# Expert products of 256 columns, one to a quarter slot, normalisation on ScalarE, and max products ahead of the score product

## The chip, the cores and the metric

The kernel runs on one core of a Trainium2 chip. The metric is the time of one execution in device microseconds, from three runs of the kernel before. A profile is one further execution; its span is measured from the first to the last instruction.

## What is computed

x is 2048 x 256 in float32. Four layers follow each other, each of them on a normalised x and added to x:

```python
x = x + xcond_attention(layernorm(x), ctx, ctx, tau, delta)      # 16 heads of 16, 2048 queries, 1601 keys
x = x + moe_top1(layernorm(x))                                    # 8 experts of 256x256, top one, times its probability
x = x + local_attention(ctx, layernorm(x), lenS2, p_t)            # window of 256 keys, tanh([context, x] @ W_c.T)
x = x + slot_layer(layernorm(x))                                  # router to 64 slots (top 8), GRU, slot attention
def moe_top1(x):
    probs = softmax(x @ router_w.T + router_b)
    top1, weights = argmax(probs), max(probs)
    y_all = einsum('bsd,eod->bseo', x, expert_w) + expert_b
    return y_all[top1] * weights
def layernorm(x): return (x - mean(x)) / sqrt(var(x) + 1e-5)
```

## The kernel before

The 2048 tokens are worked on in four chunks of 512 (four tiles of 128). For each chunk the attention of the first layer runs through 52 **slots**: four groups of four heads, and in each group 13 blocks of up to 128 keys. A slot has four **quarters**, one for each head, so a chunk has 208 quarters. In each quarter TensorE computes a score product into one of two PSUM banks (L977, bf16, 512 columns), ScalarE takes its exponential (L616), and one or two **max products** (L735, bf16, 401 columns) of the next group are computed, whose row maxima VectorE takes (L1125) from a ring of three PSUM banks. The max of a row of scores is subtracted later through two extra rows of the score product. Five max products fall on most slots. At the end of a slot TensorE computes the products of the probabilities of the slot before with the values (`pv`, L814, float32, four at a time on 32 columns each). A score product waits until the exponential two quarters before has left its bank; a max product waits until the reduction three before is done.

The rest of the layers (attention output, router, experts, local attention, slot router) is the **work behind**: the generator `behind(c - 1)` of each engine, which is woven between the quarters of chunk c. So chunk 0 carries none, chunks 1 to 3 carry that of chunks 0 to 2, and that of chunk 3 runs alone after the loop, which is called the tail here. `JOBS` is a table of numbers that sets where each product of it stands: name, the job it follows, the lag in quarters, and how many quarters its PSUM bank is held. `places()` turns it into a quarter for each job (`AT`), since all these jobs share two PSUM banks in turn. A step `yield AT[...] + n` on an engine means: go on when the loop has come to that quarter. On TensorE the work behind stands after the score product and the max products of its quarter, on VectorE after the reductions of the quarter, on ScalarE after the exponential. Each engine runs its own instructions strictly in the order written.

Jobs by name: `ota`, `otb` turn the attention output, `y0`, `y1` are its output products; `t1a`, `t1b` turn the normalised x (tile `xn`) for the router and the experts, `t2a`, `t2b` for the local attention, `t3a`, `t3b` for the slot router; `e0` to `e15` are the expert products, two experts for one tile of tokens each (L880), which VectorE adds with the gate as a factor (L1254), at four and five quarters after the job's place; `gateT` and `gb0`, `gb1` add the experts' biases; `score0`, `score1`, `z0`, `z1` belong to the local attention; `h` has a Gelu on ScalarE, `logits`, `slots` and `alphaT` belong to the slot router. Two more jobs are fixed: `o` (turning the head outputs, at quarters 6, 58, 110, 162) and `m` (turning the maxima, at 45, 97, 149, 201).

A normalisation takes statistics on VectorE (L1199, L1203), the factor 1/sqrt(var + eps) on GpSimd (`rsqrt`, L524 and L526), and then four VectorE instructions that write `xn` (L1117, `normal`), all four in one quarter.

## Time and profile before

| | us |
|---|---|
| median of three runs | 1205.0 |
| lowest, highest | 1202.1, 1208.08 |
| the profiled execution | 1201.54 |
| its span | 1199.9 |
| TensorE, VectorE, ScalarE, GpSimd busy | 1021.9, 809.4, 562.3, 44.1 |

The profiled execution took 1201.54 us, of which 1.6 us lie outside its span, and is 3.5 us under the median. The start (loading, projections, the first maxima) takes 146 us, chunk 0 takes 167 us, chunks 1 to 3 take 239 to 241 us each, and 165 us come after them. A matmul of 512 columns in float32 shows as two records of TensorE. Busy times of overlapping records are counted once.

### The profile page before, as it was taken

The numbers are of one execution on the slowest core, as the hardware profiler recorded it, in microseconds if no ns is written. First come the engines' busy times: TensorE is split into PE (matmuls) and PEld (weight loads), VectorE is DVE, ScalarE is ACT, GpSimd is POOL, SyncE is SP. The second block draws the span as 40 slices with busy tenths as digits, with TensorE's granted clock in tenths as the row PEclk, the third lists the DMA queues.
The fourth block names the chain that finished last, engine by engine and source line by source line (L and its number), as shares of the span: only waits on it lengthen the run. The fifth ranks groups of instructions, "written<-read, shape, count | busy, mean of one in ns | idle before, by whom it ended". The sixth has DMA issues, their size and how long they took to land.

```text
span 1199.9 us, 13638 instructions
## 1 busy us (share of the span) xinstructions
PE 1021.9 (85%) x4812; PEld 411.0 (34%) x4812; DVE 809.4 (67%) x1820; ACT 562.3 (47%) x1019; POOL 44.1 (4%) x54
## 2 busy tenths in 40 slices
PE   6446999999988998988899989888999898696656
PEld 3322233232333333433433334333333343243424
DVE  4446978787767777777677777776777677644232
ACT  4121066667644545666445556664455466301210
POOL 3110000000000000000000000000000000100000
PEclk9876599999989999999899999998999899978665
DMA  8996000000100000001000000010000000100512
GB/s 248 146 112 220 1 1 14 15 1 14 33 1 14 1 14 1 14 1 49 1 14 1 14 1 14 1 49 1 14 1 14 1 15 1 49 0 1 146 49 70
DMA packets 44238, 40.65 MB, mean 34 GB/s; under 512 B 10109, under 2 KB 42334, under 8 KB 43914
## 3 DMA queue, kind: packets, MB, share of 16 engines
q1 hardware_dynamic: 41594, 38.17, 13.6%
q10 hardware_dynamic: 2496, 1.35, 0.8%
q8 instruction: 38, 0.62, 0.2%
q0 software_dynamic: 80, 0.26, 0.2%
q14 instruction: 30, 0.25, 0.1%
HBM read 29.52 MB, written 10.59 MB: 33 GB/s over the span
## 4 chain that ended last, share of the span: by engine, by line
issue 46%; PE 26%; DVE 11%; DMA 6%; SPq 5%; ACT 2%; DVEq 2%; POOL 2%; POOLq 0%; ACTq 0%
DVE mx L1125 8%; PE ps_o L814 7%; PE ps_e L977 7%; PE ps_m L735 6%; DMA k_parts<-alphaT 2%; SPq L395 2%; DMA k_stack<-q_stack 2%; DMA xres<-in_x 1%; SPq L443 1%; PE ps_m L1040 1%; ACT probs L616 1%; PE ps_m L926 1%; SPq L419 1%; PE ps_m L929 1%; DMA x<-xres 1%
## 5 line engine op out<-in xcount | busy, mean ns | idle before, releaser
L1125 DVE TENSOR_REDUCE mx<-ps_m 128x1 f32<-128x401 f32 x1102 | 578.0, 568 | 203.7 <-PE ps_m L735 196.2
L616 ACT ACTIVATE probs<-ps_e 128x512 f32<-128x512 f32 (+1 forms) x832 | 472.6, 597 | 405.6 <-PE ps_e L977 404.8
L735 PE MATMUL ps_m<-k_stack,q_stack 99*128 99x401 bf16 x1102 | 356.7, 353 | 40.8 <-DVE mx L1125 40.0
L977 PE MATMUL ps_e<-q_stack,k_stack 101*128 101x512 bf16 (+1 forms) x832 | 326.2, 392 | 8.3 <-ACT probs L616 6.2
L814 PE MATMUL ps_o<-probs,v_heads 128*32 128x512 f32 (+1 forms) x1664 | 226.9, 618 | 0.0
L977 PEld LDWEIGHTS ps_e<-q_stack,k_stack 101*128 101x128 bf16 (+1 forms) x832 | 82.6, 99 | 302.1 <-ACT probs L616 207.5
L735 PEld LDWEIGHTS ps_m<-k_stack,q_stack 99*128 99x128 bf16 x1102 | 109.9, 100 | 175.9 <-DVE mx L1125 124.8
L880 PE MATMUL ps_m<-expert_w,xnT 128*128 128x512 f32 x256 | 130.8, 612 | 16.2 <-DVE xb L1254 16.2
L1254 DVE SCALAR_TENSOR_TENSOR xb<-ps_m,hot,xb 128x256 f32<-128x256 f32 x112 | 54.1, 483 | 18.3 <-PE ps_m L880 9.2
L880 PEld LDWEIGHTS ps_m<-expert_w,xnT 128*128 128x128 f32 x256 | 47.7, 196 | 48.3 <-DVE xb L1254 24.7
L814 PEld LDWEIGHTS ps_o<-probs,v_heads 128*32 128x32 f32 (+1 forms) x1664 | 33.0, 108 | 64.7 <-issue 56.1
L626 ACT COPY xnT<-ps_m 128x512 f32<-128x512 f32 x24 | 14.1, 586 | 48.7 <-PE ps_m L832 48.7
L832 PE MATMUL ps_m<-ident,xn 128*128 128x128 f32 x96 | 20.5, 321 | 17.4 <-DVE xn L1117 17.4
L524 POOL TENSOR_TENSOR var_e<-mv,eps 128x4 f32<-128x4 f32 x16 | 3.2, 199 | 698.3 <-DVE mv L1203 651.8
L763 PE MATMUL ps_m<-expert_w,probs 128*128 128x256 f32 (+1 forms) x52 | 13.8, 419 | 14.6 <-DVE v_heads L1087 14.6
L832 PEld LDWEIGHTS ps_m<-ident,xn 128*128 128x128 f32 x96 | 15.5, 170 | 23.4 <-DVE xn L1117 18.6
L723 PE MATMUL ps_e<-probs,expert_w 128*128 128x512 f32 (+1 forms) x32 | 14.5, 601 | 9.8 <-DMA probs<-in_ctxT 9.6
L552 POOL TENSOR_TENSOR xres<-xres,bo 128x1024 f32<-128x1024 f32 x4 | 9.4, 2355 | 357.6 <-DMA xres<-in_x 357.6
L926 PE MATMUL ps_m<-win_v,work 128*128 128x256 f32 x64 | 19.6, 400 | 1.9 <-ACT work L626 1.9
L842 PE MATMUL ps_m<-win_k,xnT 128*128 128x256 f32 x64 | 18.3, 422 | 2.1 <-issue 1.4
L929 PE MATMUL ps_m<-wc,xnT 128*128 128x256 f32 x64 | 19.1, 392 | 0.0
L723 PE MATMUL ps_e<-xnT,expert_w 128*128 128x512 f32 x32 | 16.3, 657 | 3.1 <-ACT xnT L597 3.1
(215 smaller groups left out, 617.3 us busy)
## 6 DMA issues: line engine op xcount, KB each, us to landing
q_stack<-q_parts SPq DMA_DIRECT2D x114, 64.0 KB, 2.2
k_stack<-k_parts SPq DMA_DIRECT2D x18, 256.0 KB, 14.0
q_parts<-attn_chunk SPq DMA_DIRECT2D x6, 384.0 KB, 5.8
...
```

The costliest lines, as they stand in the source:

```text
L395: eng.dma_start(qst[16 * (j + i):16 * (j + i) + 16, g, :, :], src.rearrange("(h e) t -> e h t", h=HG))\
L616: act.activation(probs[0:n, k % 2, h, :], ps_e[h % 2][0:n, :], ACT.Exp).then_inc(s["exp_done"], 1)
L723: mm = pe.matmul(ps_e[m][:, 0:n], wqkv[:, w, k, P * m:P * m + P], src[:, k, at_col:at_col + n], start=(k == 0), stop=(k == KT - 1))
L735: pe.matmul(ps_m[:, (UNITS * n1 + u) % RING, 0:SPLIT], qst[0:MAX_ROW, g, h, P * t:P * t + P], kst[0:MAX_ROW, HG * g + h, QUARTER_START[q]: ...
L814: mm = pe.matmul(ps_o[32 * h:32 * h + 32, :], v_sb[0:n, st, HG * g + h, :], probs[0:n, k % 2, h, :], start=(st == 0), stop=(st == ST - 1))
L832: mm = pe.transpose(bank(name, c)[:, P * t:P * t + P], src[:, t, P * k:P * k + P], ident[:])
L880: mm = pe.matmul(bank(name, c), xnT[:, k, P * t:P * t + P], expert_w[:, k, CT * j:CT * j + CT], start=(k == 0), stop=(k == KT - 1))
L926: pe.matmul(o, aT[:, k, tok:tok + P], win_v[:, k, :], start=(k == 0), stop=False)
L929: mm = pe.matmul(o, xnT[:, k, tok:tok + P], wc[:, KT + k, :], start=False, stop=(k == KT - 1))
L977: pe.matmul(ps_e[h % 2][0:n, :], kst[0:ROWS, HG * g + h, P * st:P * st + n], qst[0:ROWS, g, h, :], start=True, stop=True).then_inc(s["qk_r ...
L1125: dve.tensor_reduce(mx[:, q, col:col + 1], ps_m[:, (UNITS * n1 + u) % RING, 0:SPLIT], AX.X, ALU.max)\
L1254: last = dve.scalar_tensor_tensor(out=xb[:, t, :], in0=bank(f"e{i}", c)[:, D * (e % 2):D * (e % 2) + D], scalar=hot8[:, t, e:e + 1], in1=( ...
```

## The change

The numbers of `JOBS` are new, and so are these parts:

- On TensorE the max products of a quarter stand ahead of its score product, not behind it, and the work behind comes after the score product.
- An expert job was two float32 products of 512 columns, at its quarter and two quarters later. It is now four of 256 columns, in four quarters in a row. `y0`, `y1`, `score0`, `score1` were two products in each of two quarters, and are now one in each of four.
- `gb0` and `gb1` stand after `e2` (before: after `e15`), and VectorE adds their result there, to `xa` for the tiles whose experts have not begun. The statistics for the second normalisation of a tile are taken as soon as its four expert jobs are added.
- The three normalisations of the work behind write `xn` on ScalarE: out = Identity(rstd * x + off), two instructions in each of two quarters, the first pair three quarters ahead of `t1a`, `t2a` and `t3a`. The offset -mean * rstd is computed by GpSimd in three more instructions after the factor. The statistics of the first and third stand one in each quarter rather than two.
- The work behind of a chunk may reach into the next one: `AT` goes up to 216, and quarters from 208 on are carried out in the next chunk's first quarters.

```diff
-JOBS = [("ota", None, 10, 3), ("otb", "ota", 2, 3), ("y0", "otb", 3, 3), ("y1", "y0", 2, 3), ("t1a", "y1", 11, 3),
-        ("t1b", "t1a", 2, 3), ("router", "t1b", 3, 2), ("e0", "router", 5, 6)]
-JOBS += [(f"e{i}", f"e{i - 1}", 4, 6) for i in range(1, 4)] + [("gateT", "e3", 3, 3), ("e4", "gateT", 1, 6)]
-JOBS += [(f"e{i}", f"e{i - 1}", 4, 6) for i in range(5, NE)]
-JOBS += [("gb0", f"e{NE - 1}", 4, 4), ("gb1", "gb0", 2, 4), ("t2a", "gb1", 11, 3), ("t2b", "t2a", 2, 3),
-         ("score0", "t2b", 3, 3), ("score1", "score0", 2, 3), ("aTa", "score1", 13, 3), ("aTb", "aTa", 2, 3),
-         ("z0", "aTb", 3, 9), ("z1", "z0", 8, 9), ("t3a", "z1", 20, 3), ("t3b", "t3a", 2, 3), ("h", "t3b", 3, 5),
-         ("logits", "h", 6, 2), ("slots", "logits", 14, 6), ("alphaT", "slots", 4, 3)]
+JOBS = [("ota", None, 9, 3), ("otb", "ota", 2, 3), ("y0", "otb", 3, 6), ("y1", "y0", 4, 6), ("t1a", "y1", 16, 3),
+        ("t1b", "t1a", 2, 3), ("router", "t1b", 3, 2), ("e0", "router", 4, 6), ("e1", "e0", 4, 6), ("gateT", "e1", 4, 3),
+        ("e2", "gateT", 1, 6), ("gb0", "e2", 4, 4), ("gb1", "gb0", 2, 4), ("e3", "gb1", 2, 6)]
+JOBS += [(f"e{i}", f"e{i - 1}", 4, 6) for i in range(4, NE)]
+JOBS += [("t2a", f"e{NE - 1}", 13, 3), ("t2b", "t2a", 2, 3),
+         ("score0", "t2b", 3, 6), ("score1", "score0", 4, 6), ("aTa", "score1", 13, 3), ("aTb", "aTa", 2, 3),
+         ("z0", "aTb", 3, 9), ("z1", "z0", 8, 9), ("t3a", "z1", 21, 3), ("t3b", "t3a", 2, 3), ("h", "t3b", 3, 5),
+         ("logits", "h", 6, 2), ("slots", "logits", 12, 6), ("alphaT", "slots", 4, 3)]
 
...
     fixed = sorted([(q, q + 3) for q in O_AT] + [(q, q + 2) for q in M_AT])
+    fixed += [(HG * SLOTS + q, HG * SLOTS + end) for q, end in fixed]
...
         for q in range(HG * SLOTS):
+            if c >= 2:
+                order += [(name, c - 2) for name in AT if AT[name] == HG * SLOTS + q]
             if c:
...
-        if c:
-            order += [(name, c - 1) for name in AT if AT[name] >= HG * SLOTS]
+    order += [(name, NC - 2) for name in AT if AT[name] >= HG * SLOTS]
...
+            def shift():
+
+                pool.tensor_tensor(mean_2[:], mv[:, :, 0], neg_half[:], ALU.mult)
+                pool.drain()
+                pool.tensor_tensor(mean_2[:], mean_2[:], rstd[:], ALU.mult)
+                pool.drain()
+                pool.tensor_tensor(off[:], mean_2[:], mean_2[:], ALU.add).then_inc(s["off_ready"], 1)
+
...
+                    shift()
...
+            def normal(src, at, n):
+
+                for t in range(TT):
+                    yield at + t // 2
+                    if t == 0:
+                        act.wait_ge(s["off_ready"], n)
+                    last = act.activation(xn[:, t, 0:D], src[:, t, :], ACT.Identity, bias=off[:, t:t + 1],
+                                          scale=rstd[:, t:t + 1])
+                last.then_inc(s["xn_ready"], 1)
+
...
+                yield from normal(xa, AT["t1a"] - 3, 3 * c + 1)
...
+                yield from normal(xb, AT["t2a"] - 3, 3 * c + 2)
...
+                yield from normal(xres, AT["t3a"] - 3, 3 * c + 3)
...
-                work = begin(behind(c - 1)) if c else None
+            def chunk(c, work):
+                old, work = work, begin(behind(c - 1)) if c else None
...
                         exp(c, k, h)
+                        go_on(old, HG * (SLOTS + k) + h)
                         go_on(work, HG * k + h)
-                go_on(work, NEVER - 1)
-
+                return work
...
                 for i, t in enumerate(tiles):
-                    if i:
-                        yield AT[name] + i
                     for k in range(KT):
+                        yield AT[name] + KT * i + k
                         mm = pe.matmul(bank(name, c)[:, D * i:D * i + D], rows[:, k, P * t:P * t + P], weights[:, k, :],
                                        start=(k == 0), stop=(k == KT - 1))
                 filled(mm, name, c)
...
                     bank_free(pe, name, c)
-                    for k in range(KT):
-                        yield AT[name] + 2 * k
-                        mm = pe.matmul(bank(name, c), xnT[:, k, P * t:P * t + P], expert_w[:, k, CT * j:CT * j + CT],
-                                       start=(k == 0), stop=(k == KT - 1))
+                    for n in range(2):
+                        for k in range(KT):
+                            yield AT[name] + KT * n + k
+                            mm = pe.matmul(bank(name, c)[:, D * n:D * n + D], xnT[:, k, P * t:P * t + P],
+                                           expert_w[:, k, CT * j + D * n:CT * j + D * n + D],
+                                           start=(k == 0), stop=(k == KT - 1))
                     filled(mm, name, c)
...
-                for i in range(2):
-                    name = f"gb{i}"
-                    yield AT[name]
-                    wait_taken(pe, "gateT", c)
-                    bank_free(pe, name, c)
...
+                    for m in range(2 if i == 2 else 0):
+                        name = f"gb{m}"
+                        yield AT[name]
+                        wait_taken(pe, "gateT", c)
+                        bank_free(pe, name, c)
+                        for t in range(2):
+                            yield AT[name] + t
+                            mm = pe.matmul(bank(name, c)[:, D * t:D * t + D], gateT[:], eb[:, 2 * m + t, :],
+                                           start=True, stop=True)
+                        filled(mm, name, c)
...
                         pe.wait_ge(m_loaded[g], 32 * (c + 1))
                     for h in range(HG):
+                        for j, u in units_at(k, h):
+                            max_unit(u, c, j)
                         need(pe, s["exp_done"], HG * SLOTS * c + HG * k + h - 1)
                         pe.matmul(ps_e[h % 2][0:n, :], kst[0:ROWS, HG * g + h, P * st:P * st + n],
                                   qst[0:ROWS, g, h, :], start=True, stop=True).then_inc(s["qk_ready"], 1)
-                        for j, u in units_at(k, h):
-                            max_unit(u, c, j)
+                        go_on(old, HG * (SLOTS + k) + h)
                         go_on(work, HG * k + h)
...
-                    if t % 2 == 0:
-                        yield at + t // 2
+                    yield at + t
                     dve.bn_stats(bst[:, t, :], src[:, t, :])
-                yield at + 2
+                yield at + TT
...
-                yield AT["y0"] + 2
+                yield AT["y0"] + 4
                 dve.wait_ge(s["xres_ready"], c + 1)
                 take_sum(xa[:, 0:2, :], xres[:, 0:2, :], "y0", c)
-                yield AT["y1"] + 2
+                yield AT["y1"] + 4
                 take_sum(xa[:, 2:4, :], xres[:, 2:4, :], "y1", c)
-                yield AT["y1"] + 3
-                yield from spread_stats(xa, AT["y1"] + 3)
-                yield AT["t1a"] - 4
-                normal(xa, NC + 3 * c + 1)
+                yield from spread_stats(xa, AT["y1"] + 5)
...
-                dve.drain()
+                    if i == 2:
+                        yield AT["gb0"] + 3
+                        dve.drain()
+                        wait_filled(dve, "gb0", c)
+                        dve.tensor_tensor(xb[:, 0, :], xb[:, 0, :], bank("gb0", c)[:, 0:D], ALU.add)
+                        taken(dve.tensor_tensor(xa[:, 1, :], xa[:, 1, :], bank("gb0", c)[:, D:2 * D], ALU.add), "gb0", c)
+                        yield AT["gb1"] + 3
+                        take_sum(xa[:, 2:4, :], xa[:, 2:4, :], "gb1", c)
+                    if j == 3:
+                        yield AT[f"e{i}"] + 6
+                        dve.drain()
+                        dve.bn_stats(bst[:, t, :], xb[:, t, :])
+                dve.drain()
+                for t in range(TT):
+                    last = dve.bn_aggr(mv[:, t, :], bst[:, t, :])
+                last.then_inc(s["var_ready"], 1)
...
-                yield AT["t3a"] - 3
-                normal(xres, NC + 3 * c + 3)
```

The positions (`AT`) that come out of the table, in quarters of a chunk:

```
before: ota 10 otb 12 y0 15 y1 17 t1a 28 t1b 30 router 33 e0 38 e1 42 e2 48 e3 52 gateT 55 e4 58 e5 64 e6 68 ... e12 92
        e13 98 e14 102 e15 106 gb0 112 gb1 114 t2a 125 t2b 127 score0 130 score1 132 aTa 145 aTb 147 z0 150 z1 158
        t3a 178 t3b 180 h 183 logits 189 slots 203 alphaT 207
after:  ota 9 otb 11 y0 14 y1 18 t1a 34 t1b 36 router 39 e0 43 e1 49 gateT 53 e2 55 gb0 61 gb1 63 e3 65 e4 69 ... e10 93
        e11 99 e12 103 e13 107 e14 113 e15 117 t2a 130 t2b 132 score0 135 score1 139 aTa 152 aTb 154 z0 157 z1 166
        t3a 187 t3b 189 h 192 logits 198 slots 210 alphaT 216
```

How this stands in the engines' own order is shown at three places. The first is TensorE in a chunk with work behind, at an expert job, before: L977 is the score product, L735 the max product, L880 half of an expert job.

```order
L814 MATMUL ps_o<-probs,v_heads 32x512 x4
L977 MATMUL ps_e<-q_stack,k_stack 128x512
L735 MATMUL ps_m<-k_stack,q_stack 128x401
L880 MATMUL ps_m<-expert_w,xnT 128x512
L977 MATMUL ps_e<-q_stack,k_stack 128x512
L735 MATMUL ps_m<-k_stack,q_stack 128x401 x2
L977 MATMUL ps_e<-q_stack,k_stack 128x512
L735 MATMUL ps_m<-k_stack,q_stack 128x401
L880 MATMUL ps_m<-expert_w,xnT 128x512
L977 MATMUL ps_e<-q_stack,k_stack 128x512
L735 MATMUL ps_m<-k_stack,q_stack 128x401
L814 MATMUL ps_o<-probs,v_heads 32x512 x4
```

And the same engine after the change, where L764 is the max product, L1010 the score product, L909 a quarter of an expert job and L843 the product with the values.

```order
L843 MATMUL ps_o<-probs,v_heads 32x512 x4
L764 MATMUL ps_m<-k_stack,q_stack 128x401
L1010 MATMUL ps_e<-q_stack,k_stack 128x512
L909 MATMUL ps_m<-expert_w,xnT 128x256
L764 MATMUL ps_m<-k_stack,q_stack 128x401 x2
L1010 MATMUL ps_e<-q_stack,k_stack 128x512
L909 MATMUL ps_m<-expert_w,xnT 128x256
L764 MATMUL ps_m<-k_stack,q_stack 128x401
L1010 MATMUL ps_e<-q_stack,k_stack 128x512
L909 MATMUL ps_m<-expert_w,xnT 128x256
```

The last max product of a slot no longer stands between its last score product and `pv`, and the first one stands between `pv` and the first score product.

The second place is VectorE at the first normalisation of the work behind, before (L1125 is the reduction of a max product):

```order
L1125 TENSOR_REDUCE mx<-ps_m 128x1
L1203 BN_AGGR mv<-bst 128x2 x4
L1125 TENSOR_REDUCE mx<-ps_m 128x1 x2
L1117 TENSOR_SCALAR xn<-xa,mv,rstd 128x256 x4
L1125 TENSOR_REDUCE mx<-ps_m 128x1 x13
```

After, the four instructions are on ScalarE, among the exponentials (L629); `pv_done` among the waits marks the first exponential of a slot:

```order
L629 ACTIVATE probs<-ps_e 128x512 [waits qk_ready] x3
L647 ACTIVATE xn<-xa,off,rstd 128x256 [waits off_ready]
L647 ACTIVATE xn<-xa,off,rstd 128x256
L629 ACTIVATE probs<-ps_e 128x512 [waits qk_ready,pv_done]
L647 ACTIVATE xn<-xa,off,rstd 128x256 x2
L629 ACTIVATE probs<-ps_e 128x512 [waits qk_ready] x3
```

One pair stands between two slots, the other after the first exponential of a slot.

The third place is ScalarE at the Gelu of job `h`, before, with L616 as the exponential:

```order
L616 ACTIVATE probs<-ps_e 128x512 [waits qk_ready,pv_done]
L616 ACTIVATE probs<-ps_e 128x512 [waits qk_ready] x3
L672 ACT_TABLE_LOAD
L672 ACTIVATE hT<-ps_m,hbias 128x512 [waits bank_filled1]
L616 ACT_TABLE_LOAD [waits qk_ready]
L616 ACTIVATE probs<-ps_e 128x512 [waits pv_done]
```

After, with L698 as the Gelu:

```order
L629 ACTIVATE probs<-ps_e 128x512 [waits qk_ready,pv_done]
L698 ACT_TABLE_LOAD
L698 ACTIVATE hT<-ps_m,hbias 128x512 [waits bank_filled1]
L629 ACT_TABLE_LOAD
L629 ACTIVATE probs<-ps_e 128x512 [waits qk_ready] x3
```

The Gelu with its two table loads stood between two slots, and stands now after the first exponential of one. The number of table loads is unchanged.

## Rows read from the trace of the kernel before

**Rows 1.** The page, first part: busy time, share, instructions of each engine.

```profile
PE 1021.9 (85%) x4812; PEld 411.0 (34%) x4812; DVE 809.4 (67%) x1820; ACT 562.3 (47%) x1019; POOL 44.1 (4%) x54
```

**Rows 2.** Timeline, ScalarE: first exponential of chunk 2, and the loop's end.

```profile
554.80 0.60 ACT L616 ACTIVATE probs<-ps_e 128x512 f32<-128x512 f32 x1 [0.80 <-PE ps_e L977]
...
1035.43 0.58 ACT L680 COPY alphaT<-ps_m 64x512 f32<-64x512 f32 x1
```

**Rows 3.** Timeline of a light slot (chunk 0): start, duration, engine, line, idle before.

```profile
213.93 2.17 ACT L616 ACTIVATE probs<-ps_e 128x512 f32<-128x512 f32 x4 [0.95 <-PE ps_e L977]
...
215.07 0.39 PE L977 MATMUL ps_e<-q_stack,k_stack 101*128 101x512 bf16 x1
...
215.56 1.06 PE L814 MATMUL ps_o<-probs,v_heads 128*32 128x512 f32 x8
...
216.56 0.39 PE L977 MATMUL ps_e<-q_stack,k_stack 101*128 101x512 bf16 x1
...
217.05 2.17 ACT L616 ACTIVATE probs<-ps_e 128x512 f32<-128x512 f32 x4 [0.95 <-PE ps_e L977]
```

**Rows 4.** Timeline, ScalarE: first exponentials of slots full of expert, then of z products.

```profile
640.23 0.60 ACT L616 ACTIVATE probs<-ps_e 128x512 f32<-128x512 f32 x1 [0.95 <-PE ps_e L977]
...
644.79 0.60 ACT L616 ACTIVATE probs<-ps_e 128x512 f32<-128x512 f32 x1 [0.95 <-PE ps_e L977]
...
731.81 0.59 ACT L616 ACTIVATE probs<-ps_e 65x512 f32<-65x512 f32 x1 [1.40 <-PE ps_e L977]
...
736.38 0.60 ACT L616 ACTIVATE probs<-ps_e 128x512 f32<-128x512 f32 x1 [1.39 <-PE ps_e L977]
```

**Rows 5.** Windows of chunk 2: length, busy PE, PEld, DVE, ACT, POOL, granted clock.

```profile
576.00:601.20 25.20, 21.96 (x113) 8.97 (x111) 17.45 (x46) 12.27 (x24) 1.22 (x2) 0.86 0.00 0
692.60:710.80 18.20, 15.30 (x86) 6.10 (x85) 13.74 (x33) 9.93 (x18) 1.21 (x2) 1.00 0.00 0
```

**Rows 6.** Timeline at the first normalisation of the work behind, VectorE and TensorE.

```profile
581.55 1.38 DVE L1117 TENSOR_SCALAR xn<-xa,mv,rstd 128x256 f32<-128x256 f32 x4 [0.53 <-POOL rstd L526]
...
583.47 0.34 PE L735 MATMUL ps_m<-k_stack,q_stack 99*128 99x401 bf16 x1 [1.84 <-DVE mx L1125]
```

**Rows 7.** Timeline at expert job e4, which waits for its bank.

```profile
622.44 0.48 DVE L1254 SCALAR_TENSOR_TENSOR xb<-ps_m,hot,xb 128x256 f32<-128x256 f32 x1
...
622.98 1.13 PE L880 MATMUL ps_m<-expert_w,xnT 128*128 128x512 f32 x2 [1.50 <-DVE xb L1254]
```

**Rows 8.** Timeline, ScalarE, around the Gelu: last exponential before, first ones after.

```profile
768.78 0.60 ACT L616 ACTIVATE probs<-ps_e 128x512 f32<-128x512 f32 x1 [0.23 <-PE ps_e L977]
...
772.69 1.09 ACT L616 ACTIVATE probs<-ps_e 128x512 f32<-128x512 f32 x2
```

**Rows 9.** Groups of instructions by form, ScalarE: shapes, count, busy us, mean ns.

```profile
L654 ACT ACTIVATE work<-work,st 128x256 f32<-128x256 f32 x16 | 7.9, 494 | 0.0
...
L585 ACT ACTIVATE work<-ps_e,qk_bias,tau 128x512 f32<-128x512 f32 x8 | 6.2, 777 | 9.9 <-PE ps_e L723 9.9
...
L585 ACT ACTIVATE work<-ps_e,qk_bias 128x512 f32<-128x512 f32 x6 | 4.1, 682 | 3.0 <-DVE alphaT L1056 2.5 <-DVE win_i L1075 0.5
```

**Rows 10.** Timeline of the tail: a normalisation, then the second one's statistics.

```profile
1047.78 0.20 POOL L524 TENSOR_TENSOR var_e<-mv,eps 128x4 f32<-128x4 f32 x1 [3.74 <-DVE mv L1203]
1048.12 1.02 POOL L526 TENSOR_TENSOR rstd<-var_e,neg_half 128x4 f32<-128x4 f32 x1
1049.17 1.38 DVE L1117 TENSOR_SCALAR xn<-xa,mv,rstd 128x256 f32<-128x256 f32 x4 [1.47 <-POOL rstd L526]
...
1091.85 1.40 DVE L1199 BATCH_NORM_STATS2 bst<-xb 128x6 f32<-128x256 f32 x4
```

**Rows 11.** Timeline of the tail: float32 products of 256 columns back to back.

```profile
1117.94 0.84 PEld L929 LDWEIGHTS ps_m<-wc,xnT 128*128 128x128 f32 x4
1118.15 1.03 PE L929 MATMUL ps_m<-wc,xnT 128*128 128x256 f32 x4
...
1119.02 1.03 PE L926 MATMUL ps_m<-win_v,work 128*128 128x256 f32 x4
```

54 lines of the change are left out of this document (26 added, 28 removed).

## The prediction

> **What bounds the kernel now.** I read the page's first part, then the starts of ScalarE's exponentials (one for each quarter, so they give every slot's length), then the timeline of single slots. TensorE is the busiest engine, at 85% of the span, with VectorE at 67% and ScalarE at 47% [rows 1]. No share tells what an edit is worth, since three kinds of slot lie behind it.
>
> A **light slot** (chunk 0, and those of later chunks that carry nothing) takes 3.12 us, from one first exponential to the next [rows 3]. It is a chain: the last score product waits for the exponential two quarters back, 0.49 us later `pv` starts, 1.00 us after that comes the first score product, 0.49 us later its exponential, and two exponentials later the chain closes. ScalarE idles 0.95 us in each, so none of the engines is full.
>
> A **full slot** takes 4.56 us with two expert products of 512 columns and 4.57 us with four z products of 256 columns [rows 4]. Here TensorE never waits. The float32 passes do 0.87 us for four records of 256 columns at full clock [rows 11], so 0.43 us a product and 1.72 us a slot, whether it is two long products or four short ones.
>
> A **stalled slot** is one in which an engine does a burst. Chunks 2 and 3 together take 480.6 us, 240.3 each [rows 2]. I summed the two kinds of slot over a chunk by what each quarter carries and got 207 us, so about 33 us of a chunk are stalls: TensorE waiting for VectorE or ScalarE, and half clock after such waits. These 33 us, three times, are what the change can move. What lies before the loop stays.
>
> **Expert products in quarters: nothing.** A full slot is 4.56 us with either form [rows 4]. The stalls of this part come from elsewhere: where `o` or `m` breaks the row of jobs, the next expert job uses the bank that VectorE empties one quarter before. e4 waits so for 1.50 us [rows 7], its idle time is paid in full, and five such places (e2, e4, e5, e13, gb0) cost about 8.5 us a chunk by the slots' lengths. The new table has six (e1, e2, gb0, e3, e11, e14). I price each by the VectorE work between the slot's first max product and the emptying (0.5 us for a reduction or an addition, 0.8 for the division of the attention output): 0.6, 1.65, 1.4, 0.9, 1.9 and 1.4 us, with bias sums and clock 8.9 in all. So -0.35 us, a loss, between 3 better and 3 worse.
>
> A rule speaks against this part. Before it, the row: four z products' weight loads of 0.21 us lie inside the running passes, which follow each other at 0.22 us [rows 11]. The Trainium skill, page "TensorE: Matmul & The Clock Gate", section "The mechanism" under packing, says that a weight load overlaps a running matmul only if it goes to other rows of the array. By that, 256 more loads of 0.21 us would stand open, 54 us. The row contradicts it for this very shape, and the sum goes by the row.
>
> **Normalisation: the gain.** The four VectorE instructions stand in one quarter, 1.38 us, and TensorE waits 1.84 us for the ring behind them [rows 6]. The five slots from 576.0 take 25.2 us at a granted clock of 0.86 [rows 5]; by their content (two light, the four turns, the router, half an expert job) they would take 18.4. Of the 6.8 us, statistics and copies keep about 3.2 in the new order. On ScalarE an instruction on 256 columns with one operand per row takes 494 ns, and a second such operand adds 95 ns (777 against 682) [rows 9]; consecutive ones overlap by about 0.09, so 0.50 us each and 1.0 a pair. The pair between two slots lies in the 0.95 us that ScalarE idles [rows 3]; the pair after the first exponential pushes the chain by 1.0. Gain 3.8 us a chunk (2 to 6). At the second one the four slots from 692.6 take 18.2 us [rows 5] against 14.6 by content; its statistics go into full slots, where VectorE has room. One pair's 1.0 and the copies remain: gain 1.2 (0 to 2.5). At the third the pairs stand in quarters 0 and 1, neither between slots, and GpSimd's factor and three more instructions (2.7 us from statistics to offset, by 0.34 for each start [rows 10]) leave three quarters just enough: a loss of 0.6 (-1.5 to +0.5).
>
> **The Gelu.** From the last exponential before it to the next one pass 3.9 us [rows 8], 3.3 of them two table loads and the Gelu. Between slots 0.95 is hidden. After the first exponential of a slot nothing is: a loss of 0.8 us a chunk (0.5 to 2, if the longer wait lowers the clock).
>
> **Order and places.** With the max product ahead, the first one (0.18 us) lies between `pv` and the score product, and the last one (0.17 of the 0.49) leaves the other end; with the two of quarter 1 ahead of its score product the second exponential is 0.04 later. Sum +0.02 us a light slot (-0.05 to +0.06): +1.3 us for chunk 0. In chunks 1 to 3 a product in quarter 0 now pushes the second exponential by its whole 0.43 us and not by 0.29. With that, the contents of a chunk sum to 208.2 us against 207: -1.2 a chunk. The output products, one a quarter, gain 0.4 of the DVE's lag, but `ota` a quarter earlier waits for the division of the same slot, 0.9: -0.5.
>
> **The ledger of a wrapped chunk**: +3.8 + 1.2 - 0.6 - 0.8 - 0.35 - 1.2 - 0.5 = +1.55, and +0.45 for the half clock in 0.86's neighbours, since chunks 1 and 3 have slots there up to 1 us longer: +2.0 us, three times **-6.0 us**.
>
> **Behind the loop.** In the tail everything is open. The offset adds 0.95 us (three starts of 0.34 less overlap) and the four ScalarE instructions take 2.07 against 1.38 [rows 9, 10]: +1.65 us each time. At the second, the 1.40 us of statistics shrink to one of four [rows 10] and the bias sums leave the end, against two products and their sums among the expert jobs: +1.0. Sum **+4.3 us** (3 to 6). The slot products of chunk 2's work now run after the last quarter: **+0.5**.
>
> **Sum**: -6.0 + 1.3 + 4.3 + 0.5 = +0.1 us on the profiled 1201.5, so no change. The profiled execution is 3.5 us under the median of 1205.0, and the same ratio on the median gives **1205 us**, with 1199 to 1211 as this case's own range. About 0.5% (6 us) is what a measurement can tell from no change.
>
> **Rivals.** (1) *Faster*: the bursts were the root of more than their own slots, and ScalarE hides both pairs. Then the first two stretches fall to 0.8 us above content (6.0 and 2.8 gained), the third loses nothing, and the bank waits gain 1. Per chunk 6.0 + 2.8 - 0.8 + 1.0 - 1.7 = 7.3, three times -22, plus 6.1: -16 us, 1189; half way, 1193. For it: a wait of 1.84 us of TensorE [rows 6] in a stretch whose clock is 0.86 [rows 5], so one burst costs twice. Against it: VectorE keeps its statistics and additions. Chance 0.33 for anything under 1199, with 1193 its middle.
> (2) *Slower*: ScalarE runs its instructions in order, and the wait for the offset stands among the exponentials. It decides as soon as the statistics end less than 2.7 us before ScalarE gets there. VectorE is late by an addition or a normalisation of the heads, ScalarE then stops, score products stop, and max products behind them. At 1 us of wait and both pairs open, 1.9 us more at nine places, +17 us: 1218 on the profiled execution, 1222 on the median, and 1214 with half of the places. For it: only three or four quarters lie between. Against it: when VectorE is late, the ring of three holds TensorE and so ScalarE back too. Chance 0.22.
> (3) *Half clock after the Gelu*: TensorE idles some 2.7 us there; if the clock halves as after the wait of rows 6, 3.4 to 6.8 us at half speed, 1.5 to 3 us, three times, 1209 to 1214. Chance 0.08, half of it beyond 1211.
> (4) The edits do nothing: the order of the instructions shows them moved, so this is only the case that stalls wander whole, which my forecast holds. Open weight loads, by the rule above, 1255: 0.02.
>
> My own sum has 0.35. So faster 0.33, same 0.39 (0.35 and half of (3)), slower 0.28. The range of eight in ten takes in most of (1) and part of (2): 1189 to 1219.
>
> **What would show it.** Chunk 0 at 168 to 169 us, light slots of 3.14; full slots of 4.57 with records of 256 columns; the stretch of the first normalisation at about 21 us with clock near 1; ScalarE instructions for `xn` of 0.59 us; a Gelu slot near 8 us; waits for L1254's bank at six places; the tail 4 us longer. A light slot over 3.2 or under 3.0 us would move chunk 0 by more than 3 us and break the sum; so would waits on the offset over 0.5 us, or the loss of the bank waits.

## The result and the profile after

The changed kernel takes **1240.2 us** (median of four runs, 1235.6 to 1241.93), beside it the kernel before 1206.54 us (1202.1 to 1208.21): 1.0281 times as long, 95% interval 1.0249 to 1.0314. Forecast were 1205 us and a range of 1189 to 1219. The loss is outside both.

I read the profile of after in the order of the prediction. First the starts of ScalarE's exponentials (start, duration, engine, line, operation, what it waited for), to hold against [rows 2] and [rows 4]: chunk 0 starts at 144.60, chunk 1 at 312.10, chunk 2 at 555.08, chunk 3 at 808.02, and two neighbouring full slots with four expert products at 650.01 and 654.58.

```profile
144.60 0.60 ACT L629 ACTIVATE probs<-ps_e 128x512 f32<-128x512 f32 x1 [41.35 <-PE ps_e L1010]
312.10 1.08 ACT L629 ACTIVATE probs<-ps_e 128x512 f32<-128x512 f32 x2 [0.96 <-PE ps_e L1010]
555.08 1.08 ACT L629 ACTIVATE probs<-ps_e 128x512 f32<-128x512 f32 x2 [0.40 <-PE ps_e L1010]
650.01 0.60 ACT L629 ACTIVATE probs<-ps_e 128x512 f32<-128x512 f32 x1 [1.39 <-PE ps_e L1010]
654.58 0.60 ACT L629 ACTIVATE probs<-ps_e 128x512 f32<-128x512 f32 x1 [1.39 <-PE ps_e L1010]
808.02 1.08 ACT L629 ACTIVATE probs<-ps_e 128x512 f32<-128x512 f32 x2 [0.40 <-PE ps_e L1010]
```

So chunk 0 takes 167.5 us (before 167.4), chunk 1 243.0 (241.0), chunk 2 252.9 (239.5), chunk 3 254.1 (241.1), and what follows the last exponential 175.2 (164.4). The start is 1.8 us shorter; over the kernels of this case it ends between 144.6 and 149.9 us, so this says nothing about the change. Light and full slots are as before. Of the 37.4 us between the two spans (1237.3 and 1199.9), 26 lie in chunks 2 and 3 and 10.8 in the tail.

Next the same stretches of chunk 2, cut at slots 0, 6, 12 and 17, then slots 36, 44, 48 and the end, first before and then after. Columns: stretch and its length, busy time of TensorE, its weight loads, VectorE, ScalarE and GpSimd, each with its instructions, then the granted clock of TensorE (1.00 is 2.4 GHz, 0.50 is 1.2 GHz), the busy share of the DMA and its GB/s.

```profile
554.80:579.80 25.00, 23.30 (x131) 9.56 (x130) 17.87 (x38) 14.81 (x27) 2.36 (x1) 1.00 0.09 31
579.80:609.60 29.80, 27.11 (x136) 10.86 (x134) 20.83 (x54) 14.78 (x28) 1.22 (x2) 0.89 0.00 1
609.60:635.70 26.10, 22.52 (x107) 8.19 (x107) 17.21 (x35) 12.03 (x23) 0.00 (x0) 1.00 0.06 16
...
723.40:757.40 34.00, 32.14 (x182) 14.67 (x180) 25.04 (x57) 20.70 (x37) 1.21 (x2) 1.00 0.05 12
757.40:775.80 18.40, 16.09 (x94) 6.92 (x93) 12.01 (x25) 13.13 (x21) 0.00 (x0) 1.00 0.00 1
775.80:794.30 18.50, 15.94 (x83) 4.75 (x82) 14.76 (x42) 10.39 (x21) 0.00 (x0) 1.00 0.09 22
```

```profile
555.10:588.60 33.50, 30.18 (x143) 11.86 (x141) 19.04 (x40) 15.88 (x28) 2.34 (x1) 0.85 0.10 34
588.60:614.80 26.20, 23.32 (x137) 9.69 (x136) 19.18 (x52) 16.46 (x31) 1.79 (x5) 1.00 0.01 1
614.80:645.40 30.60, 27.64 (x120) 11.90 (x119) 17.59 (x36) 12.29 (x22) 0.00 (x0) 0.83 0.05 14
...
732.50:768.50 36.00, 32.31 (x182) 14.89 (x181) 24.47 (x54) 22.86 (x46) 0.00 (x0) 1.00 0.04 12
768.50:786.80 18.30, 15.16 (x77) 4.79 (x76) 12.56 (x30) 11.87 (x22) 1.77 (x5) 0.91 0.00 1
786.80:808.00 21.20, 18.39 (x87) 7.37 (x88) 13.76 (x40) 13.41 (x23) 0.00 (x0) 0.84 0.06 17
```

The first normalisation (second row) gained 3.6 us. Slots 0 to 5 lost 8.5, slots 12 to 16 lost 4.5, slots 36 to 43 lost 2.0, slots 48 to 51 lost 2.7. Where it lost most, the clock column fell. Summed over chunks 1 to 3, TensorE ran at half clock for 30.7 us before and for 85.3 us after, 51 of these in five pieces of 10.2 us. An estimate from these two figures: the 54.6 us more cost at most half of their length, 27.3 us, and chunks 1 to 3 together lost 28.4. Three of the pieces:

```profile
558.60:568.80 10.20, 10.20 (x33) 2.98 (x35) 3.42 (x7) 3.18 (x6) 2.34 (x1) 0.50 0.15 51
633.70:643.90 10.20, 10.20 (x31) 4.11 (x34) 4.41 (x9) 2.90 (x5) 0.00 (x0) 0.50 0.00 0
794.10:800.90 6.80, 6.66 (x25) 3.07 (x26) 2.39 (x6) 3.71 (x7) 0.00 (x0) 0.50 0.00 0
```

What did TensorE do ahead of each? The timeline of after has a wait each time, in brackets. Ahead of 558.6 the slot products (L990) wait for the last VectorE step of alpha (L1366); these products were carried into the next chunk. Ahead of 633.7 the bias sums `gb0` (L926) wait for their bank, which VectorE empties (L1284) behind the division of the attention output (L1219). Around 794.1 the Gelu stands on ScalarE between two table loads, and `logits` (L982) wait for it.

```profile
557.22 0.43 DVE L1366 TENSOR_TENSOR work<-work,st 128x256 f32<-128x256 f32 x1
557.70 0.65 PE L990 MATMUL ps_m<-xn,work 128*64 128x257 f32 x2 [1.57 <-DVE work L1366]
...
630.16 0.42 DVE L1219 TENSOR_TENSOR attn_chunk<-ps_m,z_inv 128x256 f32<-128x256 f32 x1
630.67 0.48 DVE L1284 SCALAR_TENSOR_TENSOR xb<-ps_m,hot,xb 128x256 f32<-128x256 f32 x1
631.30 0.67 PE L926 MATMUL ps_m<-expert_b_tiles,gateT 32*128 32x256 f32 x2 [1.22 <-DVE xb L1284]
...
793.50 0.69 ACT L698 ACTIVATE hT<-ps_m,hbias 128x512 f32<-128x512 f32 x1
794.21 1.28 ACT L629 ACT_TABLE_LOAD   x1
794.24 1.97 PE L982 MATMUL ps_m<-w,hT 128*128 128x64 f32 x8 [1.61 <-ACT hT L698]
```

In the tail TensorE's three waits for `xn` grew by 4.0 us. The slot products carried over from the last chunk of the loop stand open there too: of the two waits in the last row the shorter one, 2.2 us, is theirs. Waits of TensorE in the tail, first before and then after (us in total, times, longest):

```profile
PE ps_m L832 <- DVE xn L1117: 17.4, 3, 6.2
PE ps_m L959 <- DVE work L1329: 4.9, 1, 4.9
```

```profile
PE ps_m L861 <- ACT xn L647: 21.4, 3, 7.7
PE ps_m L990 <- DVE work L1366: 7.2, 2, 5.0
```

### The profile page after: what moved, and what is told of

It is laid out like the page before. It is cut to its first block, busy times and chain, and to the rows that moved or that the text cites. A ratio compares the mean times of both kernels' runs of the same rounds, so it can differ in the third digit from the quotient of the medians.

```text
span 1237.3 us, 14226 instructions
## 1 busy us (share of the span) xinstructions
PE 1051.3 (85%) x5068; PEld 473.5 (38%) x5068; DVE 800.7 (65%) x1776; ACT 592.6 (48%) x1067; POOL 50.9 (4%) x90
## 4 chain that ended last, share of the span: by engine, by line
issue 61%; PE 18%; DMA 6%; DVE 5%; SPq 3%; ACT 2%; POOL 2%; POOLq 1%; DVEq 1%; ACTq 0%
PE ps_o L843 5%; PE ps_m L764 5%; PE ps_e L1010 5%; DVE mx L1159 4%; SPq L399 1%; DMA k_stack<-q_stack 1%; DMA xres<-in_x 1%; DMA k_parts<-attn_chunk 1%; PE ps_m L1074 1%; SPq L447 1%; POOL rstd L530 1%; DMA x<-xres 1%; POOL xres L564 1%; DMA qk_bias<-in_L_bk 1%; ACT probs L629 1%
## 5 line engine op out<-in xcount | busy, mean ns | idle before, releaser
L629 ACT ACTIVATE probs<-ps_e 128x512 f32<-128x512 f32 (+1 forms) x832 | 478.9, 597 | 400.7 <-PE ps_e L1010 399.5
L764 PE MATMUL ps_m<-k_stack,q_stack 99*128 99x401 bf16 x1102 | 364.2, 360 | 25.2 <-DVE mx L1159 24.3
L1010 PE MATMUL ps_e<-q_stack,k_stack 101*128 101x512 bf16 (+1 forms) x832 | 329.6, 396 | 9.0 <-ACT probs L629 8.1
L764 PEld LDWEIGHTS ps_m<-k_stack,q_stack 99*128 99x128 bf16 x1102 | 108.8, 99 | 336.4 <-DVE mx L1159 217.9
L843 PE MATMUL ps_o<-probs,v_heads 128*32 128x512 f32 (+1 forms) x1664 | 230.7, 628 | 0.0
L909 PE MATMUL ps_m<-expert_w,xnT 128*128 128x256 f32 x512 | 149.9, 394 | 13.9 <-DVE xb L1284 13.9
L1010 PEld LDWEIGHTS ps_e<-q_stack,k_stack 101*128 101x128 bf16 (+1 forms) x832 | 84.5, 102 | 85.0 <-ACT probs L629 49.8
L909 PEld LDWEIGHTS ps_m<-expert_w,xnT 128*128 128x128 f32 x512 | 100.4, 199 | 42.4 <-DVE xb L1284 18.7
L1284 DVE SCALAR_TENSOR_TENSOR xb<-ps_m,hot,xb 128x256 f32<-128x256 f32 x112 | 54.2, 484 | 20.2 <-PE ps_m L909 10.5
L843 PEld LDWEIGHTS ps_o<-probs,v_heads 128*32 128x32 f32 (+1 forms) x1664 | 33.2, 109 | 66.8 <-issue 47.6
L792 PE MATMUL ps_m<-expert_w,probs 128*128 128x256 f32 (+1 forms) x52 | 13.8, 419 | 14.4 <-DVE v_heads L1121 14.4
L647 ACT ACTIVATE xn<-xb,off,rstd 128x256 f32<-128x256 f32 x16 | 8.6, 590 | 32.4 <-POOL off L538 32.1
L990 PE MATMUL ps_m<-xn,work 128*64 128x257 f32 x32 | 15.1, 612 | 10.3 <-DVE work L1366 10.3
L870 PE MATMUL ps_m<-win_k,xnT 128*128 128x256 f32 x64 | 21.0, 435 | 2.6 <-issue 1.9
L752 PE MATMUL ps_e<-xnT,expert_w 128*128 128x512 f32 x32 | 18.3, 722 | 4.6 <-ACT xnT L610 4.6
```

The lines of the kernel that those rows point to most:

```text
L629: act.activation(probs[0:n, k % 2, h, :], ps_e[h % 2][0:n, :], ACT.Exp).then_inc(s["exp_done"], 1)
L752: mm = pe.matmul(ps_e[m][:, 0:n], wqkv[:, w, k, P * m:P * m + P], src[:, k, at_col:at_col + n], start=(k == 0), stop=(k == KT - 1))
L764: pe.matmul(ps_m[:, (UNITS * n1 + u) % RING, 0:SPLIT], qst[0:MAX_ROW, g, h, P * t:P * t + P], kst[0:MAX_ROW, HG * g + h, QUARTER_START[q]: ...
L843: mm = pe.matmul(ps_o[32 * h:32 * h + 32, :], v_sb[0:n, st, HG * g + h, :], probs[0:n, k % 2, h, :], start=(st == 0), stop=(st == ST - 1))
L870: mm = pe.matmul(bank(name, c)[:, D * i:D * i + D], rows[:, k, P * t:P * t + P], weights[:, k, :], start=(k == 0), stop=(k == KT - 1))
L909: mm = pe.matmul(bank(name, c)[:, D * n:D * n + D], xnT[:, k, P * t:P * t + P], expert_w[:, k, CT * j + D * n:CT * j + D * n + D], start=( ...
```

## The experiments

Theory A: the waits are about as long as I summed them, but some set off half clock, at places where there was none, and the tail pays for ScalarE's normalisation. Rivals: one part costs everywhere (the order of the products, the quartered jobs), or half clock falls by chance. "Slots 12 to 16" and the like are from the exponentials' starts. All ratios are to the kernel before, timed beside the run. All clock figures and slot lengths come from one profiled execution of each kernel.

**Fillers at two waits, then two places moved.** Four products whose result is overwritten stand ahead of TensorE's waits for alpha and for the Gelu (e1); the slot products two quarters later (e2); the Gelu three quarters later, between two slots (e3). The table carries e3's shift on: `logits` and, as in e2, the slot products stand two quarters later there too.

```diff
+                for _ in range(4):
+                    pe.matmul(bank("slots", c)[:, 0:D], xnT[:, 0, 0:P], win_k[:, 0, :], start=True, stop=True)
                 pe.wait_ge(s["alpha_ready"], c + 1)
...
-        ("logits", "h", 6, 2), ("slots", "logits", 12, 6), ("alphaT", "slots", 4, 3)]
+        ("logits", "h", 6, 2), ("slots", "logits", 14, 6), ("alphaT", "slots", 4, 3)]
...
-                yield AT["h"] + 4
+                yield AT["h"] + 7
```

> The changed kernel with work added: ahead of the wait for alpha (job slots) and ahead of the wait for the Gelu (job logits) TensorE computes four products of 256 columns into the bank that the job then overwrites, 1.7 us at full clock, so that it is not idle there; both waits stay. Theory A (the loss is mostly half clock that an idle TensorE brings on): the first two slots of chunks 2 and 3 fall from 7.8 and 7.4 us to about 5 and 4.2, the Gelu slot from 8.2 to 6.5 to 7; some 15 us less, about 1225. Theory B (the loss is the waits' own length): nothing is gained and the added products cost up to 2 us a chunk, 1240 to 1246.

> The changed kernel with one number changed: the slot products stand 14 quarters behind the logits, not 12 (before: 14). Theory A: the 1.8 us wait for alpha goes and with it the half clock over the next two or three slots, 6 us in each of chunks 2 and 3 and 2 to 3 us behind the loop: about 1225. Theory B: only the wait itself goes, 1.8 us at three places: about 1235.

> The changed kernel with the Gelu seven quarters behind job h, not four, so that it stands after the last exponential of a slot again, and the logits eight behind, not six. Theory A: the Gelu slot loses 0.8 us of open wait and the half clock over the next slots, 3 to 4 us a chunk: about 1230. Theory B: 0.8 us a chunk: 1238.

Measured: e1 1.0203 (1.0171 to 1.0235), e2 1.0264 (1.0219 to 1.0309), e3 1.0225 (1.0181 to 1.0268). Half clock in chunks 1 to 3 fell from 85.3 to 61.4, 68.3 and 51.2 us.

With the fillers slots 0 and 1 took 11.0 and 10.6 us in chunks 2 and 3, from 15.2, at or near full clock. TensorE is busy up to the product that it waited for:

```profile
561.50 1.95 PE L990 MATMUL ps_m<-win_k,xnT 128*128 128x256 f32 x8
563.38 0.65 PE L994 MATMUL ps_m<-xn,work 128*64 128x257 f32 x2
```

Added work made the stretch 4 us shorter. That shows that the clock costs more here than the wait's own 1.57 us; e1's time lies nearer to theory A (some 1225 us) than to B. e2 took 3.5 us off slots 0 to 5: slots 0 and 1 fell to 9.1, slots 2 to 5 rose from 18.3 to 20.9, all of it at full clock. Its time of 1235.1 is theory B's, and its interval overlaps with that of the changed kernel. e3 brought slots 48 to 51 of chunks 2 and 3 from 21.2 and 20.1 to 17.9 and 16.9, while slots 0 to 5 stayed at 33.1 and 31.6 (from 33.5). Its time is near theory A's, but a part of the gain can be that of e2.

**Normalisation on VectorE again, in the changed table** (e4: no offset, `normal` at three quarters ahead of each turn).

> The changed kernel with the three normalisations of the work behind on VectorE again, four instructions in one quarter, three quarters ahead of the turning product; GpSimd's offset is left out. Theory A with my sum of this part: the bursts come back (3 to 4 us a chunk more at the first), the third normalisation's ScalarE slot (6.6 to 7.7 us) falls by 2 to 3, and the part behind the loop is 4 to 5 us shorter: 1237 to 1242. Rival C (the move to ScalarE is what made the kernel slow): back by 15 us or more, under 1225.

1.0151 (1.011 to 1.0193), 1221.5 us: that is the rival's side (under 1225), and theory A is out. The tail takes 165.3 us. TensorE's waits for `xn` in the tail are back at 16.8, and slots 44 to 47 are at 15.5 (from 18.3 to 19.6). Slots 6 to 11 stay at 25.8: the 3.6 us gained there are not ScalarE's alone.

```profile
PE ps_m L857 <- DVE xn L1147: 16.8, 3, 6.2
```

**Three parts alone, on the kernel before.** e5: max products ahead of the score product; e6: expert jobs in four quarters; e7: the normalisations on ScalarE, two instructions in each of two quarters, at two (third: three) quarters ahead of the turns.

```diff
+                        for j, u in units_at(k, h):
+                            max_unit(u, c, j)
                         need(pe, s["exp_done"], HG * SLOTS * c + HG * k + h - 1)
...
-                        yield AT[name] + 2 * k
...
+                            yield AT[name] + KT * n + k
...
+                yield from normal(xa, AT["t1a"] - 2, 3 * c + 1)
```

> The kernel before with one edit: in each quarter the products for the maximum stand ahead of the score product. Theory A (the change's own sum on this part: +0.02 us a light slot, later second exponentials in wrapped chunks): chunk 0 goes from 167.4 to 168 to 169 us, each wrapped chunk by 0 to 1.5 us, the whole by 1 to 5 us, ratio 1.001 to 1.004. Rival C (the order of issue is what costs, since a score product held back behind two max products delays every exponential): chunk 0 stays near 168, but each wrapped chunk grows by 4 us or more, ratio 1.01 or more.

> The kernel before with one edit: each expert product of 512 columns is issued as two of 256, one in each of four quarters. Theory A: a full slot stays at 4.56 to 4.57 us, the expert stretches of the chunks stay within 1 us, ratio 0.997 to 1.003. Rival B (weight loads stand open, as a page of the Trainium skill has it): 256 more loads of 0.21 us, +54 us, ratio 1.04. Rival C (the bank emptied one quarter before is waited for at each expert job, since its first product now fills the bank later): +1 us at each of five places in three chunks, ratio 1.01.

> The kernel before with one edit: the three normalisations of a chunk's later work go to ScalarE, with the offset from GpSimd, two instructions in each of two neighbouring quarters, the table of places unchanged. Theory A (from the run that took ScalarE's normalisations out of the changed kernel and gained 17 us, 10 of them behind the loop): the same edit alone costs 12 to 20 us here, 8 to 11 of them behind the last exponential (164.4 to 173 to 175 us), the rest as waits for the offset in the loop; ratio 1.010 to 1.017. Rival D (the move only costs where the changed table puts it): the tail still grows by 3 to 5 us, the loop gains 2 to 4 us a chunk at the first normalisation, ratio 0.993 to 1.0.

e5: 1.0002 (0.998 to 1.0024), chunk 0 167.2 us. e6: 0.996 (0.9939 to 0.9981); open weight loads would have cost 54 us. e7: 1.0081 (1.0057 to 1.0104), its tail 170.5 (+6.1), its three wrapped chunks +3.4 us together, with 3 us gained in slots 6 to 11 of each chunk and as much lost behind them. So neither the order nor the quarters cost anything, and ScalarE's normalisation alone costs 10 us, between theory A (12 to 20) and rival D (none).

**Where `gb0` stands.** Three tables that are equal from the second normalisation's turns on, with `gb0` at quarter 61 (e9), 62 (e13) and 63 (e8). From the changed kernel to e9 only that later half moves, by two quarters, the carried slot products with it. Between e9, e13 and e8 not only `gb0` moves but `gb1` and the expert jobs from `e3` on as well.

```diff
-        ("e2", "gateT", 1, 6), ("gb0", "e2", 4, 4), ("gb1", "gb0", 2, 4), ("e3", "gb1", 2, 6)]
+        ("e2", "gateT", 1, 6), ("gb0", "e2", 8, 4), ("gb1", "gb0", 2, 4), ("e3", "gb1", 2, 6)]
...
-JOBS += [("t2a", f"e{NE - 1}", 13, 3), ("t2b", "t2a", 2, 3),
+JOBS += [("t2a", f"e{NE - 1}", 15, 3), ("t2b", "t2a", 2, 3),
```

> The changed kernel with one number other: the first product of the experts' bias sums (gb0) stands two quarters later, at quarter 63 and not 61, and all that follows by up to two quarters later. Theory A (TensorE waits 1.2 us at quarter 61 for the bank that VectorE empties behind the division, and 10.24 us of half clock follow that wait): the wait goes, the slots 12 to 16 of a chunk fall from 30.6 to 26 to 27 us, three times 4, less about 2 us for later work: ratio to the kernel before 1.017 to 1.022 against the changed kernel's 1.028. Rival E (the half clock follows from the low activity of the slot itself, bias products with 32 rows and the turn of o): slots 12 to 16 stay at 29 to 31 us and half clock stands there still, ratio 1.026 to 1.032.

> The changed kernel with one number other: the second normalisation's turns (t2a) stand 15 quarters behind the last expert job and not 13, so that everything from there on stands at the places of the run with gb0 two quarters later, while gb0 itself stays at quarter 61. Theory A (of the 27 us that the run with gb0 later gained, about half is the bank wait with its half clock, and half the later places: the third normalisation's pairs between the slots, the Gelu one slot on): slots 12 to 16 stay at 30.6 us, slots 44 to 47 fall from 18.3 to 19.6 to 15.5 to 16.1, slots 48 to 51 from 20.5 to 18 to 19, so 4 to 5 us a chunk: 1223 to 1230, ratio 1.017 to 1.023. Rival F (nearly all of it was the bank wait): ratio 1.025 or more.

> The changed kernel with gb0 at quarter 62, one later than in the changed kernel and one earlier than in the run with gb0 at 63; from the second normalisation's turns on, all stands as in both runs with the later half. So the three kernels differ in the place of the bias sums and the expert jobs behind them alone. Theory A (a wait of TensorE at this place sets off the half clock): at 62 the bank is empty about one quarter's time, 0.6 us, sooner as TensorE sees it, so the wait shrinks from 1.2 to 0.3 to 0.8 us and the half clock shrinks or goes; slots 12 to 16 at 26 to 29 us, ratio 1.009 to 1.014. Rival E (the wait only moves with the bank and half clock follows just the same): slots 12 to 16 at 30 to 31 us, ratio 1.017 as in the run with gb0 at 61.

e9 1.0173 (1.014 to 1.0207), e13 1.0123 (1.0069 to 1.0177), e8 1.0088 (1.0051 to 1.0125). So the later half is worth about 13 us (in chunks 2 and 3 slots 44 to 47 at 15.5, 48 to 51 at 18.9 and 17.0), and `gb0` at 63 another 10; both are clear of the intervals. e8 gained more than either of its theories had. e13's interval overlaps with both neighbours, so its times alone decide nothing. Slots 12 to 16 of chunk 2 in e9 and in e13, which issue the same work:

```profile
617.60:648.20 30.60, 27.64 (x120) 11.82 (x119) 17.59 (x36) 12.29 (x22) 0.00 (x0) 0.83 0.05 14
```

```profile
608.90:634.60 25.70, 22.83 (x119) 9.85 (x117) 17.27 (x36) 12.24 (x22) 0.00 (x0) 1.00 0.06 16
...
625.35 0.67 PE L926 MATMUL ps_m<-expert_b_tiles,gateT 32*128 32x256 f32 x2 [0.64 <-DVE xb L1284]
```

The wait fell from 1.2 to 0.64 us, the stretch by 4.9. So 4.3 us went that are not the wait's own length; the clock column has 0.83 for the one and 1.00 for the other. But e8, with no wait at L926, has the same half clock in one chunk of three, behind a wait of 1.03 us for a max product's ring at 625.46:

```profile
608.60:627.20 18.60, 15.82 (x88) 7.01 (x86) 13.01 (x27) 9.87 (x18) 0.00 (x0) 1.00 0.08 22
627.20:637.40 10.20, 10.20 (x32) 3.03 (x25) 3.53 (x7) 2.39 (x4) 0.00 (x0) 0.50 0.00 0
```

That ring wait stands just ahead of quarter 63 in all nine chunks of e8, e10 and e14, and 10 us or more of half clock in two of them (e14's is below).

**Towards a kernel that beats both.** e10: e8 with VectorE's normalisation. e11 and e12 start from the kernel before with quartered expert jobs: e11 spreads the first statistics and moves the turns by a quarter, e12 has ScalarE's normalisation at the first place alone and in the loop alone. e14 is e10 with the end of the later work done inside its own chunk. e15 is e10 with `gb0` at 62.

```diff
-        ("e2", "gateT", 1, 6), ("gb0", "e2", 4, 4), ("gb1", "gb0", 2, 4), ("e3", "gb1", 2, 6)]
+        ("e2", "gateT", 1, 6), ("gb0", "e2", 8, 4), ("gb1", "gb0", 2, 4), ("e3", "gb1", 2, 6)]
...
-                yield from normal(xa, AT["t1a"] - 3, 3 * c + 1)
...
+                yield AT["t1a"] - 3
+                normal(xa, NC + 3 * c + 1)
```

> The changed kernel with gb0 two quarters later and the three normalisations back on VectorE (at three quarters ahead of the turns). Theory A (the costs are apart: places of gb0 and later, and ScalarE's normalisation behind the loop): the tail falls from 176.2 to 165 us, the loop stays, ratio 0.998 to 1.002 to the kernel before. Rival G (they overlap, since the later places already hide ScalarE's pairs, and VectorE's normalisation of 1.4 us now makes TensorE wait): ratio 1.003 to 1.007.

> The kernel before with expert products in quarters and, at the first normalisation alone, one statistics instruction in each of four quarters, the turns one quarter later; normalisation stays on VectorE, the second statistics stay as before; the third turns one quarter earlier, so that the chunk's work still ends inside its chunk. Theory A (the gain at the first normalisation is that of the places, since it came with VectorE too): slots 6 to 11 fall from 29.8 to 26 to 27 us, slots 12 to 16 stay at 26: three times 3, ratio 0.987 to 0.992. Rival H (it takes the y products in quarters and the longer lag): slots 6 to 11 stay at 29 us or more, ratio 0.994 to 0.998.

> The kernel before with expert products in quarters and ScalarE's normalisation at the first place only and in the loop only; behind the loop VectorE normalises as before. Theory A (at this place ScalarE's idle time hides both pairs, as slots 6 to 11 of 26.6 us showed with all three moved, and the cost of the move lay at the other two places and behind the loop): slots 6 to 11 at 26.6 us, slots 12 to 16 at 26 to 27.7, tail 164, ratio 0.987 to 0.993. Rival I (the gain is taken back in slots 12 to 16 and by the clock): ratio 0.994 or more.

> The run with gb0 two quarters later and VectorE's normalisation (1197 us, ratio 0.994), with one edit: what is left of a chunk's later work (the slot products and the turn of alpha) is done at the end of the chunk and not carried into the next chunk's first three slots. Theory A (the carried jobs meet the next chunk's ota and otb there: slots 0 to 5 take 33.2 to 36.4 us against 24.1 in chunk 1, which has nothing carried, so 9 to 12 us twice): slots 0 to 5 return to 24 to 25 us in chunks 2 and 3, and the flush costs 5 to 7 us at the end of chunks 1, 2 and 3 (where the last one is paid already): ratio 0.984 to 0.990. Rival J (the flush brings its own half clock and costs as much as the carrying): ratio 0.992 to 0.998.

> The changed kernel with gb0 one quarter later (62), the later half two quarters later, and the three normalisations back on VectorE: the three undone parts together. Theory A (the costs are additive, and a wait of 0.6 us at gb0 sets off no half clock): slots 12 to 16 at 25.5 to 26 us at full clock in all three chunks, the loop 5 to 12 us shorter than in the kernel with gb0 at 63 and VectorE's normalisation, tail 165 to 171 us; ratio 0.985 to 0.993. Rival K (the kernel with gb0 at 63 and VectorE already has all of it, and half clock falls at random places): ratio 0.993 to 0.998.

| | ratio, 95% interval | half clock, chunks 1 to 3 | slots 12 to 16, chunks 1 to 3 |
|---|---|---|---|
| e10 | 0.9944 (0.991 to 0.9977) | 27.3 | 25.5, 25.5, 27.0 |
| e11 | 1.0092 (1.0056 to 1.0129) | 71.7 | 24.7, 24.7, 24.7 |
| e12 | 0.9952 (0.9929 to 0.9974) | 30.7 | 25.8, 27.2, 27.4 |
| e14 | 0.9958 (0.9927 to 0.9989) | 37.5 | 25.5, 32.2, 25.5 |
| e15 | 1.0057 (1.004 to 1.0075) | 54.6 | 25.8, 25.8, 30.0 |

e10 beats the kernel before by 0.6% and the changed one by 3.3%, more than either of its theories had, though its tail of 170.7 us is 5 over what I expected. e6, e12 and e14 beat the kernel before by 0.4 to 0.5%; none of the four is shown to be better than the others. e12 gains nothing beyond e6, as rival I had it. e11 misses both its theories: slots 6 to 11 gained 0.8 to 3.2 us, but the whole table slid by one quarter and `gb0` with it, from 112 to 113, three quarters behind `o`. There it waits as in the changed kernel, and half clock follows, in each of the three chunks:

```profile
938.89 0.67 PE L898 MATMUL ps_m<-expert_b_tiles,gateT 32*128 32x256 f32 x2 [1.43 <-DVE xb L1256]
...
930.00:940.30 10.30, 8.87 (x51) 4.15 (x48) 7.72 (x17) 4.97 (x10) 0.00 (x0) 1.00 0.00 1
940.30:950.50 10.20, 10.20 (x33) 2.56 (x31) 4.77 (x9) 3.20 (x6) 0.00 (x0) 0.50 0.00 0
```

e14 gave slots 0 to 5 of chunks 2 and 3 their 24.1 us back (from 33.2 and 36.4, 21.4 together). It paid 14.4 of them in slots 48 to 51 of chunks 1 and 2 (25.2 and 26.0, from 17.9 and 18.9), and 6.7 more went to half clock in slots 12 to 16 of chunk 2. So there is no gain over e10, and the ratio is the one of rival J. e15 met neither theory. At `gb0` it did as said in two chunks, but in the third half clock stood there behind the same wait, and slots 0 to 5 took 36.2 and 33.9 us. These parts do not add up.

## Why the prediction was wrong

**Held.** Light slots, chunk 0 (167.5 for 168 to 169), full slots (4.57, e6), the weight loads hidden, ScalarE's `xn` at 0.59 us, 3.6 us gained at the first normalisation (3.8). e7 shows ScalarE to be good for it, e4 shows the new places to be so too. The waits for the offset, rival 2, are 1.9 us in chunks 1 to 3, the longest 1.0 (first row: total, times, longest). In the second row, of the first normalisation over the whole program, 590 is the mean ns of one, and 8.8 us is the wait for the offset, nearly all of it in the tail:

```profile
ACT xn L647 <- POOL off L538: 1.9, 3, 1.0
...
L647 ACT ACTIVATE xn<-xa,off,rstd 128x256 f32<-128x256 f32 x16 | 8.6, 590 | 9.2 <-POOL off L538 8.8
```

**The term that failed: bank waits at -0.35 us a chunk.** The waits themselves are as I had them, or shorter. `gb0`'s was priced at 1.4 us and is 1.22 in each of the three chunks; e1, e2, e11 and e14 wait 0.7, 1.0, 1.3 and 1.1 us in chunk 2, and e3 does not wait. Together they are 5.4 us, against 5.5 of the five places before; the 8.9 and 8.5 of the prediction hold more than the waits. The step that failed is that I held six waits against five as if a wait cost its own length and it did not matter where it stands. At quarter 61 slots 12 to 16 took over 29 us, where 25.5 to 26 is the undisturbed length, in 17 of 18 chunks of six kernels (after, e1 to e4, e9); with `gb0` at 62 in one of six (e13, e15), at 63 in two of nine (e8, e10, e14). So it is not chance alone, the last of the rivals above. The half clock adds some 4.5 us a chunk, 13 in three. The prediction had that mechanism, as rival 3, but at the Gelu alone and with 3.4 to 6.8 us of half clock; the longest pieces are 10.2 us and stand behind waits that I had priced already. Why quarter 61 brings it is not shown: the kernel before waits 1.50 us for `e4`'s bank, at quarter 58 [rows 7], in each of its chunks 1 to 3, and the clock stays at 1.00 there (its slots 12 to 16 above, 26.1 us).

**The carried work: +0.5 us once.** I counted the products behind the last quarter, and not that in chunks 2 and 3 they meet `ota`, `otb` and the wait for alpha. There slots 0 to 5 took 8.5 us more, twice. In e2 they ran wholly at full clock and took 30.0 us, still 5.0 more than before: so the larger part is the work itself and its waits, and 3.5 the clock and the place. Where the work stays carried, the runs took at most 4.6 of the 8.5 away (e1). e14, which carries nothing, took all of it away and paid 7 us for it at the end of a chunk.

**Gelu and third normalisation: -0.8 and -0.6.** Slots 48 to 51 lost 1.9, 2.7 and 3.2 us, half clock included: the term was two to four times too small, though inside its upper bound of 2 in one chunk only. Slots 44 to 47 lost 0.4, -0.1 and 1.2 us, so -0.6 held; but e4 and e9 show some 2.9 us to be had there, by VectorE or by pairs between the slots.

**Contents: -1.2.** Slots 36 to 43 grew by 2.0, with the clock at 1.00; the longer slots there lack no clock, and e5 gives 0.4 of it to the order. I put the rest down to the places of the jobs; no run takes it apart.

**The tail: +4.3, measured 10.8.** ScalarE's three normalisations add 4.0 us of waits, about what I had priced. In e7, which changes nothing else, the waits grow by 4.6 and the tail by 6.1 us, with 102.3 us at half clock there and not 93.0. I put the other 4.7 down to the open slot products, whose +0.5 was far too small: `pv` of the last slot runs 5.9 us behind the last exponential. But in e4, which has them too and VectorE's normalisation, the tail is only 165.3, with half clock down to 86.3 us. e10, with the same work there in nearly the same order, takes 170.7, with 92.2 us at half clock. So the 4.7 are not shown to be theirs alone, and what I left out of this sum as well is the clock.

On the rule of the Trainium skill, page "TensorE: Matmul & The Clock Gate", section "The mechanism": e6 has the 256 further loads and is no slower (0.996, where 54 us would be 1.04), so the trace stands. The same section of the Trainium skill also names a background weight buffer as a place that a load can go to ahead of a running matmul, which I left out; with it the page and e6 agree.
